# Feed-forward of a latent-attention block in two phases: the down product as one Strassen product

## The chip, the cores and the metric

The kernel runs on one core of a Trainium2 chip as a single program. The metric is the time of that program on the device in microseconds (us), as the median of several runs. A profile of one execution gives the span of its instructions, the busy time of each engine (PE is TensorE, PEld its weight loads, DVE VectorE, ACT ScalarE, POOL GpSimd) and the queue of SyncE (SP), which issues all the transfers between memory and the chip.

## What is computed

All arithmetic is float32. After the attention part the feed-forward part takes 896 rows (8 x 112) of 1,024 features:

```python
logits = jnp.einsum('bsh,he->bse', hidden_states, gate_w)
routing_weights, selected_experts = jax.lax.top_k(logits, K)
h = jax.nn.relu(jnp.einsum('bsh,hi->bsi', hidden_states, up_w)) ** 2
shared_out = jnp.einsum('bsi,ih->bsh', h, down_w)
...
routed_out = jnp.einsum('bsl,lh->bsh', moe_out, fc2_w)
return _layernorm(shared_out + routed_out, ln_gamma, ln_beta)
```

`up_w` is 1,024 x 2,048 and `down_w` is 2,048 x 1,024. The attention part, the layer norm ahead of it and the expert products stand before this part and are not touched.

## The kernel before

Precision: each float32 operand is kept as two parts in a reduced format, hi (a rounded copy, written by ACT) and lo (value minus hi, written by POOL or DVE). A product is three matmuls (`three`: hi x hi, lo x hi, hi x lo) that add up in one PSUM bank, so every tile costs three matmuls per 128 features of depth.

Feed-forward, up: the 2,048 hidden features are worked off in 8 pairs (`F_PAIRS`) of 2 x 128. In each pair the up product is a Strassen product in the Winograd form: 7 units (`up_product(p, n)`, n = 0 to 6, in the order `F_BLOCKS`: A11, S2, A12, S3, S1, A22, S4), each of 12 matmuls with 448 columns (448 of the 896 rows). The weight operand of a unit is a 128 x 512 block or a sum of blocks. For one pair the work beside PE is:

- SP loads four blocks A11, A21, A22, A12 of 256 KB (`load_up`), each when the unit that last needed its buffer has its lo.
- POOL makes the four block sums in place (`up_sum`, steps 1 to 4: S1, S2, S4, S3) and the lo of all 7 units (`up_lo`), in one fixed order.
- ACT writes the hi of each unit (`up_hi`, two slots `F_UNIT`), copies the first product, and writes the rectified and the rounded hidden block.
- DVE adds the products (`up_combine`, 7 times), squares the hidden block and writes its lo.

Feed-forward, down: between the units of the next pairs PE runs the down product of finished pairs, `down_product(c, r, eh, pairs)`: for each of 7 row tiles of 128 and each half `eh` of the 1,024 outputs, 12 matmuls with 512 columns per pair, added by DVE to `Y` (`add_down`). The list `WEAVE` says how many of these groups stand behind each unit (two as a rule), so most units are followed by 24 matmuls of down work. The last two pairs' down products follow the last unit, and the layer norm of the rows runs behind them. The seven `routed_product` groups (12 matmuls with 512 columns each) stand in the first pair.

The order on each engine is written out by hand; engines wait for each other by counting semaphores, and every queue is worked off in order, SP's too.

```python
def three(out_ap, w, a, first, last):
    pe.matmul(out_ap, w[0], a[0], start=first, stop=False)
    pe.matmul(out_ap, w[1], a[0], start=False, stop=False)
    return pe.matmul(out_ap, w[0], a[1], start=False, stop=last)
```

## Time and profile before

| | |
|---|---|
| median of 3 runs (lowest to highest) | 1729.22 us (1728.54 to 1729.24) |
| the profiled execution: its time / its span | 1728.13 us / 1726.3 us |
| granted TensorE clock, mean | 0.999 of full speed |
| busy: PE / DVE / POOL / ACT | 1717.0 / 965.2 / 950.4 / 701.8 us |
| feed-forward part (first up unit to the last matmul) | about 1411 to 1719.5 us |

The span runs from the first instruction to the last; the time lies 1.83 us above it. A PE that is busy is not at its peak, since matmuls are pipelined: what counts in the text is the distance from the start of one matmul to the start of the next.

### The profile page before, as it was taken

The numbers are of one execution on the slowest core, as the hardware profiler recorded it, in microseconds if no ns is written. First come the engines' busy times: TensorE is split into PE (matmuls) and PEld (weight loads), VectorE is DVE, ScalarE is ACT, GpSimd is POOL, SyncE is SP. The second block draws the span as 40 slices with busy tenths as digits, with TensorE's granted clock in tenths as the row PEclk, the third lists the DMA queues.
The fourth block names the chain that finished last, engine by engine and source line by source line (L and its number), as shares of the span: only waits on it lengthen the run. The fifth ranks groups of instructions, "written<-read, shape, count | busy, mean of one in ns | idle before, by whom it ended". The sixth has DMA issues, their size and how long they took to land.

```text
span 1726.3 us, 24782 instructions
## 1 busy us (share of the span) xinstructions
PE 1717.0 (99%) x8599; PEld 1516.2 (88%) x8599; DVE 965.2 (56%) x1503; ACT 701.8 (41%) x1361; POOL 950.4 (55%) x779
## 2 busy tenths in 40 slices
PE   9999999999999999999999999999999999999998
PEld 8988998899999988988998898889888988888886
DVE  3611112743434357874887588657657465555568
ACT  4311212233334357743873377337613233333332
POOL 2365552445555549874767476735535245465553
PEclk9999999999999999999999999999999999999999
DMA  8788875566668758844773477334222212111124
GB/s 272 228 290 283 292 245 214 176 192 214 217 217 253 225 189 302 293 129 136 242 236 113 142 250 218 121 99 148 82 86 88 95 31 73 56 61 49 56 78 172
DMA packets 196951, 296.31 MB, mean 172 GB/s; under 512 B 19344, under 2 KB 159120, under 8 KB 195984
## 3 DMA queue, kind: packets, MB, share of 16 engines
q1 hardware_dynamic: 196880, 295.41, 52.4%
q8 instruction: 38, 0.62, 0.2%
q14 instruction: 33, 0.27, 0.0%
HBM read 197.10 MB, written 98.27 MB: 171 GB/s over the span
## 4 chain that ended last, share of the span: by engine, by line
PE 96%; DVE 2%; DMA 0%; ACT 0%; POOL 0%; issue 0%; SPq 0%; DVEq 0%; ACTq 0%; POOLq 0%
PE bank L2061 30%; PE bank L2062 29%; PE bank L2063 29%; PE bank L2285 5%; PE bank L2147 1%; DVE mid_region L1764 1%; DVE y_region L1783 0%; DMA mid_region<-k_latents_scratch 0%; PE bank L2426 0%; PE bank L2133 0%; PE bank L2104 0%; DVE tile_region L1771 0%; DVE y_region L1771 0%; POOL tile_region L994 0%; PE bank L2140 0%
## 5 line engine op out<-in xcount | busy, mean ns | idle before, releaser
L994 POOL TENSOR_TENSOR tile_region<-tile_region,small 128x487 f32<-128x487 f32 x224 | 221.1, 1024 | 72.9 <-DVE small L1647 72.7
L2061 PE MATMUL bank<-mid_region 128*128 128x488 f32 (+4 forms) x532 | 218.7, 411 | 0.1
L2062 PE MATMUL bank<-mid_region 128*128 128x488 f32 (+4 forms) x532 | 199.8, 376 | 0.0
L2063 PE MATMUL bank<-mid_region 128*128 128x488 f32 (+4 forms) x496 | 185.4, 374 | 0.0
L2061 PE MATMUL bank<-mid_region,act_region 128*125 128x512 f32 (+2 forms) x434 | 168.7, 389 | 0.1
L2062 PE MATMUL bank<-mid_region,act_region 128*125 128x512 f32 (+2 forms) x434 | 168.5, 388 | 0.0
L1271 ACT ACTIVATE tile_region<-bank,small 128x487 f32<-128x487 f32 x224 | 153.8, 687 | 30.3 <-DVE small L1651 30.3
L960 POOL TENSOR_TENSOR slab_raw<-slab_raw 128x256 f32<-128x256 f32 x128 | 98.7, 774 | 120.2 <-DMA slab_raw<-in_slabs 112.6
L1303 ACT ACTIVATE mid_region<-bank 125x512 fp32r<-125x512 f32 x224 | 136.7, 613 | 54.5 <-PE bank L2285 54.5
L1651 DVE TENSOR_REDUCE small<-bank 128x1 f32<-128x487 f32 x224 | 145.7, 652 | 20.6 <-PE bank L2063 20.6
L1702 DVE TENSOR_TENSOR mid_region<-bank,mid_region 125x512 fp32r<-125x512 f32 x224 | 151.4, 681 | 9.3 <-ACT mid_region L1303 9.3
L2063 PE MATMUL bank<-mid_region,act_region 128*125 128x512 f32 (+2 forms) x404 | 156.5, 387 | 0.0
L2285 PEld LDWEIGHTS bank<-ident,tile_region 128*125 128x125 f32 x896 | 131.4, 187 | 15.5 <-POOL tile_region L994 1.6
L978 POOL TENSOR_TENSOR slab_split<-slab_raw,slab_split 128x512 fp32r<-128x512 f32 x64 | 87.6, 1371 | 94.2 <-ACT slab_split L1221 94.2
L2285 PE MATMUL bank<-ident,tile_region 128*125 128x128 f32 x896 | 134.4, 273 | 0.8 <-DVE mid_region L1702 0.8
L2063 PE MATMUL bank<-act_region,mid_region 128*128 128x376 f32 (+3 forms) x340 | 118.4, 348 | 0.0
L1783 DVE TENSOR_TENSOR y_region<-y_region,bank 128x512 f32<-128x512 f32 x105 | 68.7, 681 | 83.0 <-PE bank L2063 82.2
L1522 DVE TENSOR_TENSOR small_region<-bank,small_region 128x375 fp32r<-128x375 f32 (+1 forms) x40 | 22.4, 563 | 161.9 <-ACT small_region L1137 161.8
L2061 PEld LDWEIGHTS bank<-mid_region 128*128 128x128 f32 (+2 forms) x532 | 100.5, 189 | 10.1 <-issue 1.9
L2062 PEld LDWEIGHTS bank<-mid_region 128*128 128x128 f32 (+2 forms) x532 | 101.1, 190 | 6.7
L2061 PE MATMUL bank<-act_region,mid_region 128*128 128x376 f32 (+3 forms) x304 | 104.9, 345 | 0.0
L2062 PE MATMUL bank<-act_region,mid_region 128*128 128x376 f32 (+3 forms) x304 | 104.1, 343 | 0.0
(256 smaller groups left out, 4351.7 us busy)
## 6 DMA issues: line engine op xcount, KB each, us to landing
slab_raw<-in_slabs SPq DMA_DIRECT2D x112, 256.0 KB, 3.6
q_scratch<-y_region SPq DMA_DIRECT2D x16, 1792.0 KB, 8.1
mid_region<-q_scratch SPq DMA_DIRECT2D x32, 896.0 KB, 6.7
slab_raw<-in_slabs SPq DMA_DIRECT2D x37, 512.0 KB, 3.5
weight_sums_scratch<-slab_raw SPq DMA_DIRECT2D x32, 512.0 KB, 4.2
v_scratch<-slab_split SPq DMA_DIRECT2D x8, 1536.0 KB, 7.8
slab_raw<-weight_sums_scratch SPq DMA_DIRECT2D x48, 256.0 KB, 4.7
mid_region<-v_scratch SPq DMA_DIRECT2D x32, 384.0 KB, 3.2
```

The lines of the kernel that those rows point to most:

```text
L960: pool.tensor_tensor(out, a, b, op).then_inc(s_sum[h], 1)
L978: pool.tensor_tensor(WB[n][1], WRAW[n], f32(WB[n][0]), ALU.subtract).then_inc(s_blo, 1)
L994: pool.tensor_tensor(PR[i][:, 0:KEYS], PR[i][:, 0:KEYS], rrow[:, i:i + 1].broadcast_to([P, KEYS]), ALU.mult).then_inc(s_pn, 1)
L1271: act.activation(PR[i][:, 0:KEYS], SB[RING[i]][:, 0:KEYS], ACT.Exp, bias=negmax[:, i:i + 1], accum_out=rowsum[:, i:i + 1]).then_inc(s_exp, 1)
L1303: act.activation(PT[0][0:KT, :, i * P:(i + 1) * P], TB[RING[i]][0:KT, :].rearrange("p (t n) -> p t n", t=4), ACT.Copy).then_inc(s_pth, 1)
L1651: dve.reduce_max(negmax[:, i:i + 1], SB[RING[i]][:, 0:KEYS], AX.X, negate=True).then_inc(s_max, 1)
L1702: dve.tensor_tensor(PT[1][0:KT, :, cols], TB[RING[i]][0:KT, :].rearrange("p (t n) -> p t n", t=4), f32(PT[0][0:KT, :, cols]), ALU.subtract ...
L1783: return dve.tensor_tensor(Y[:, r, cols_of(eh)], Y[:, r, cols_of(eh)], GB[i][:, :], op)
L2061: pe.matmul(out_ap, w[0], a[0], start=first, stop=False)
L2062: pe.matmul(out_ap, w[1], a[0], start=False, stop=False)
L2063: return pe.matmul(out_ap, w[0], a[1], start=False, stop=last)
L2285: last = pe.transpose(TB[RING[i]][0:KT, t * P:(t + 1) * P], PR[i][:, t * KT:(t + 1) * KT], ident[:, :])
```

## The change

The down product is taken out of the up phase. In phase one PE runs the 56 up units one behind the other (the seven routed groups stay in the first pair). The hidden values of all 2,048 features stay whole on chip in float32 (`HR`, eight pieces of 256 features). In phase two the down product is one Strassen product over 1,024 + 1,024 features: 7 products `D_PRODUCTS` in 4 steps `kp` each, with 4 or 3 row tiles (`D_TILES`: row tile 6 rides along as a fourth where it needs no sum), 25 tiles of 24 matmuls with 512 columns. The last tile is made in two halves of 256 columns.

What goes with it:

- The sums T1 to T4 of the down weight's blocks are made during phase one, in 16 chunks of 512 KB (`CHUNKS` gives pair, unit and buffer of each): SP loads a chunk in two transfers, DVE makes four sums of 128 x 256 one behind the other (`down_sums`), SP stores the chunk to memory. Phase two loads them as slabs of 512 KB (`load_down`, 28 slabs).
- The lo of the units S1 and A22 (n = 4 and 5) moves from POOL to DVE (`up_lo` in the vector program), counted by `s_ulo2`.
- From unit 8 on there are three slots for the hi and lo of a unit; ACT writes the hi of unit u + 3 behind unit u.
- The square of the hidden block is made by ACT in place; its hi and lo are made later, for each product of phase two (`chunk_hi`, `chunk_lo` 128 x 768, `ride_hi`, `ride_lo` 128 x 256), and DVE makes the sums S1 to S4 of the hidden values (`hidden_sum`, 128 x 768).
- ACT's `down_hi` and POOL's `down_lo` (128 x 1,024) now run 28 times in phase two, instead of 16 times in the up phase.
- DVE adds each product tile to one to four places of `Y` (`take`). The layer norm takes the row tiles in the order 3, 4, 5, 6, 0, 1, 2.

The diff, cut to its core:

```diff
-WEAVE = [[1] * 7, [0, 2, 2, 2, 2, 3, 3]] + [[2] * 7] * (F_PAIRS - 5) + [[2] * 7, [1] * 7, [1] * 7]
+ROUTED_WEAVE = (2, 2, 1, 1, 1, 0, 0)
+CHUNKS = ((1, 0, "Y"), (1, 1, "X"), (1, 3, "Z"), (1, 4, "V"), (1, 6, "Y"), (2, 0, "X"), (2, 3, "Z"), (2, 4, "V"),
+          (2, 6, "X"), (3, 0, "Y"), (3, 3, "Z"), (3, 5, "X"), (3, 6, "Y"), (4, 4, "X"), (4, 6, "Y"), (5, 5, "Y"))
+D_PRODUCTS = (("A11", "B11", 0), ("S1", "T1", 0), ("S2", "T2", None), ("A22", "T4", None), ("S3", "T3", None),
+              ("S4", "B22", 1), ("A12", "B21", 1))
+D_TILES = [(0, 1, 2) if h is None else (0, 1, 2, 3) for _, _, h in D_PRODUCTS]
...
+            def load_chunk(c):
+                buf, use, m, kp = CHUNK_BUF[c], CHUNK_USE[c], c % 4, c // 4
+                if use:
+                    sp.wait_ge(s_cst[buf], 16 * use)
+                to = CHUNK[buf].rearrange("p (e k c) -> p e k c", e=2, k=2)
+                for kh in range(2):
+                    blocks = slabs[down_base(kh):down_base(kh) + NK].rearrange("(e m) p c -> p e m c", e=2)
+                    sp.dma_start(to[:, :, kh, :], blocks[:, :, m, 2 * P * kp:2 * P * (kp + 1)]).then_inc(s_cld[buf], 16)
+            def store_chunk(c):
+                buf, use, m, kp = CHUNK_BUF[c], CHUNK_USE[c], c % 4, c // 4
+                sp.wait_ge(s_csum[buf], 4 * (use + 1))
+                sp.dma_start(td_d[:, kp, :, m, :].rearrange("t p c -> p t c"),
+                             CHUNK[buf].rearrange("p (t c) -> p t c", t=4)).then_inc(s_cst[buf], 16)
...
+                for n in range(7):
+                    u = 7 * p + n
+                    if more and n == 2:
+                        sp.wait_ge(s_ulo, lo_count(p, 3))
+                        load_up(p + 1, "A11")
+                    if more and n == 3:
+                        sp.wait_ge(s_ulo2, 2 * p + 1)
+                        load_up(p + 1, "A21")
+                    if more and n == 4:
+                        sp.wait_ge(s_ulo2, 2 * p + 2)
+                        load_up(p + 1, "A22")
+                    if more and n == 5:
+                        sp.wait_ge(s_ulo, lo_count(p, 6))
+                        load_up(p + 1, "A12")
+                    for c in range(len(CHUNKS)):
+                        if CHUNK_UNIT[c] + 2 == u:
+                            store_chunk(c)
+                        later = [i for i in range(c + 1, len(CHUNKS)) if CHUNK_BUF[i] == CHUNK_BUF[c]][:1]
+                        if CHUNK_UNIT[c] + 5 == u:
+                            for i in later:
+                                load_chunk(i)
+            sp.wait_ge(s_ulo, lo_count(F_PAIRS - 1, 3))
+            sp.wait_ge(s_ulo2, 2 * F_PAIRS - 1)
+            load_down(0)
+            sp.wait_ge(s_ulo2, 2 * F_PAIRS)
+            sp.wait_ge(s_ulo, lo_count(F_PAIRS - 1, 6))
+            for buf in "XYZV":
+                sp.wait_ge(s_cst[buf], 16 * CHUNK_BUF.count(buf))
...
             for p in range(F_PAIRS):
                 up_sum(1, p, "A21", "A21", "A22", ALU.add)
                 up_lo(p, 0)
                 up_sum(2, p, "A11", "A21", "A11", ALU.subtract)
                 up_lo(p, 1)
-                if p == 1:
-                    down_lo(0)
                 up_lo(p, 2)
                 up_sum(3, p, "A12", "A12", "A11", ALU.subtract)
                 up_sum(4, p, "A11", "A22", "A11", ALU.subtract)
                 up_lo(p, 3)
-                if 0 < p < F_PAIRS - 1:
-                    down_lo(2 * p - 1)
-                if p == F_PAIRS - 1:
-                    down_lo(2 * F_PAIRS - 4)
-                up_lo(p, 4)
-                up_lo(p, 5)
                 up_lo(p, 6)
-                if 0 < p < F_PAIRS - 2:
-                    down_lo(2 * p)
-            for d in range(2 * F_PAIRS - 3, 2 * F_PAIRS):
+            for d in range(D_SLABS):
                 down_lo(d)
...
-                if u >= 2:
+                if 2 <= u < 8:
                     act.wait_ge(s_up, u - 1)
...
+                if u > 8:
+                    act.wait_ge(s_up, u - 2)
+                act.activation(up_slot(u)[0], F_BLOCK[F_SRC[name]], ACT.Copy).then_inc(s_uhi, 1)
...
+            def hidden_block(p, n, i):
+                m, h = F_TILES[n]
+                act.wait_ge(s_upc, 7 * p + {2: 2, 4: 4, 5: 6, 6: 7}[n])
+                if i == 0:
+                    for buf, first in (("V", 3), ("Z", 4), ("X", 5), ("Y", 6)):
+                        if p == first:
+                            act.wait_ge(s_cst[buf], 16 * CHUNK_BUF.count(buf))
+                to = HR[p][:, m, h * HALF:(h + 1) * HALF]
+                act.activation(to, F_FIRST if n == 2 else F_SUM, ACT.Relu).then_inc(s_relu, 1)
+                act.wait_ge(s_relu, 4 * p + i + 1)
+                act.activation(to, to, ACT.Square).then_inc(s_sq, 1)
...
-                    if n < 5 or not last:
-                        up_hi(p + (n >= 5), (n + 2) % 7)
...
+                    for v in (u + 2,) if u < 5 else (7, 8) if u == 5 else (u + 3,):
+                        if v < UNITS:
+                            up_hi(v // 7, v % 7)
...
+                    if last and n == 5:
+                        chunk_hi(0, 0)
+                        chunk_hi(0, 1)
+                    if n in F_TILES:
+                        hidden_block(p, n, list(F_TILES).index(n))
+                    if last and n == 5:
+                        down_hi(0)
...
+            chunk_hi(0, 2)
+            ride_hi(0, 0)
+            chunk_hi(0, 3)
+            down_hi(1)
+            for kp in range(1, 4):
+                ride_hi(0, kp)
+            down_hi(2)
+            for q in range(6):
+                for kp in range(4):
+                    chunk_hi(q + 1, kp)
+                    if q == 4:
+                        ride_hi(1, kp)
+                    down_hi(4 * q + kp + 3)
+            for d in range(27, D_SLABS):
...
+            def down_sums(c):
+                buf, use = CHUNK_BUF[c], CHUNK_USE[c]
+                dve.wait_ge(s_cld[buf], 32 * (use + 1))
+                W11, W21, W12, W22 = [part(CHUNK[buf], 256 * k, 256) for k in range(4)]
+                for n, (out_, a, b) in enumerate([(W11, W12, W11), (W12, W22, W12), (W22, W22, W11), (W21, W22, W21)]):
+                    if n:
+                        dve.wait_ge(s_csum[buf], 4 * use + n)
+                    dve.tensor_tensor(out_, a, b, ALU.subtract).then_inc(s_csum[buf], 1)
...
+                    if n == (2 if p == 0 else 1):
+                        up_lo(p, 4)
+                    if n == (3 if p == 0 else 2):
+                        up_lo(p, 5)
+                    for c, r in woven(p, n):
+                        routed_rows(c, db(c), r, 1)
+                    if 7 * p + n in CHUNK_UNIT:
+                        down_sums(CHUNK_UNIT.index(7 * p + n))
+                    if p == F_PAIRS - 1 and n == 5:
+                        chunk_lo(0, 0)
+                        chunk_lo(0, 1)
...
+            chunk_lo(0, 2)
+            ride_lo(0, 0)
+            chunk_lo(0, 3)
+            for kp in range(3):
+                hidden_sum("S1", kp, "A21", "A22", ALU.add)
+            for kp in range(1, 4):
+                ride_lo(0, kp)
+            hidden_sum("S1", 3, "A21", "A22", ALU.add)
+            for kp in range(4):
+                chunk_lo(1, kp)
+                hidden_sum("S2", kp, "S1", "A11", ALU.subtract)
...
+            def down_step(q, kp, i, out_ap, ms=slice(0, 4)):
+                pe.wait_ge(s_olo, 4 * q + kp + 1)
+                pe.wait_ge(s_dlo, 4 * q + kp + 1)
+                act, rows = D_OP[4 * (q % 2) + kp], slice(i * P, (i + 1) * P)
+                if i == 3:
+                    pe.wait_ge(s_rlo, 4 * D_PRODUCTS[q][2] + kp + 1)
+                    act, rows = D_RIDE[kp], slice(0, P)
+                w = [t.rearrange("p (m k c) -> p m k c", m=4, k=2) for t in d_slot(4 * q + kp)]
+                for k in range(2):
+                    last = three(out_ap, [act[l][:, k, rows] for l in range(2)], [w[l][:, ms, k, :] for l in range(2)],
+                                 kp == k == 0, kp == 3 and k == 1)
+                return last
+            pe.wait_ge(s_upc, UNITS)
+            for q in range(6):
+                banks = DB if q % 2 == 0 else GB
+                for kp in range(4):
+                    for i in D_TILES[q]:
+                        if kp == 0 and q >= 2:
+                            pe.wait_ge(s_dtake, taken(q - 2 if i in D_TILES[q - 2] else q - 4, i))
+                        last = down_step(q, kp, i, banks[i][:, :])
+                        if kp == 3:
+                            last.then_inc(s_dmm, 1)
+                    if kp < 3:
+                        last.then_inc(s_dmm, 1)
+            for i in D_LAST[:-1]:
+                pe.wait_ge(s_dtake, taken(0, i) if i == 3 else taken(4, i))
+                for kp in range(4):
+                    last = down_step(6, kp, i, DB[i][:, :])
+                last.then_inc(s_dmm, 1)
+            pe.wait_ge(s_dtake, taken(5, 0))
+            for h, dst in enumerate((DB[2], GB[0])):
+                for kp in range(4):
+                    last = down_step(6, kp, 2, dst[:, 0:256], slice(2 * h, 2 * h + 2))
```

## Rows read from the trace of the kernel before

**Rows 1.** The page: the busy line
```profile
PE 1717.0 (99%) x8599; PEld 1516.2 (88%) x8599; DVE 965.2 (56%) x1503; ACT 701.8 (41%) x1361; POOL 950.4 (55%) x779
```

**Rows 2.** The page: the chain that ended last, by engine
```profile
PE 96%; DVE 2%; DMA 0%; ACT 0%; POOL 0%; issue 0%; SPq 0%; DVEq 0%; ACTq 0%; POOLq 0%
```

**Rows 3.** One up-phase window: length, busy of PE, PEld, DVE, ACT, POOL; clock, DMA
```profile
1600.00:1650.00 50.00, 50.00 (x235) 43.94 (x234) 28.66 (x41) 16.58 (x27) 28.74 (x20) 1.00 0.23 74
```

**Rows 4.** PE in order of time: start, duration; one unit, one down group, the end
```profile
1549.93 0.36 PE L2061 MATMUL bank<-mid_region,slab_split 128*128 128x448 f32 x1
...
1552.37 0.39 PE L2061 MATMUL bank<-small_region,slab_split 128*128 128x512 f32 x1
...
1555.10 0.36 PE L2061 MATMUL bank<-mid_region,act_region 128*128 128x448 f32 x1
...
1716.44 0.28 PE L2061 MATMUL bank<-act_region,slab_split 128*128 128x256 f32 x1
...
1719.20 0.28 PE L2063 MATMUL bank<-mid_region,act_region 128*128 128x256 f32 x1
```

**Rows 5.** POOL by line, 1420 to 1727 us: sums and lo parts (min/median/max ns)
```profile
L1078 POOL TENSOR_TENSOR slab_raw<-slab_raw x28: 1287/1296/1725, 1436.2 to 1660.6; 128x512 f32<-128x512 f32 x28
...
L1090 POOL TENSOR_TENSOR small_region<-tile_region,small_region x6: 2397/2398/2410, 1458.6 to 1637.2; 128x1024 fp32r<-128x1024 f32 x6
```

**Rows 6.** ACT and DVE by shape, 1430 to 1690 us: count, busy us, mean ns
```profile
L1419 ACT ACTIVATE slab_split<-slab_raw 128x512 fp32r<-128x512 f32 x25 | 15.7, 629 | 51.1 <-PE bank L2063 34.2 <-POOL slab_raw L1078 16.9
...
L1439 ACT ACTIVATE tile_region<-tile_region 128x448 f32<-128x448 f32 x24 | 13.8, 575 | 2.7 <-DVE tile_region L1951 2.6
...
L1429 ACT ACTIVATE mid_region<-tile_region 128x1024 fp32r<-128x1024 f32 x8 | 8.4, 1046 | 2.1 <-PE bank L2063 2.1
...
L1951 DVE TENSOR_TENSOR tile_region<-tile_region,bank 128x448 f32<-128x448 f32 x16 | 9.9, 619 | 18.0 <-PE bank L2063 12.9 <-issue 5.1
```

**Rows 7.** DMA issues, 1420 to 1700 us: KB each, median us to landing
```profile
tile_region<-in_slabs SPq DMA_DIRECT2D x15, 512.0 KB, 3.4
slab_raw<-in_slabs SPq DMA_DIRECT2D x28, 256.0 KB, 2.6
```

**Rows 8.** Hand-overs in order of time: POOL sum, ACT hi, POOL lo
```profile
1551.85 1.56 POOL L1078 TENSOR_TENSOR slab_raw<-slab_raw 128x512 f32<-128x512 f32 x1
...
1553.44 0.63 ACT L1419 ACTIVATE slab_split<-slab_raw 128x512 fp32r<-128x512 f32 x1 [2.21 <-POOL slab_raw L1078]
...
1554.15 1.29 POOL L1084 TENSOR_TENSOR tile_region_rounded<-slab_raw,slab_split 128x512 fp32r<-128x512 f32 x1 [0.74 <-ACT slab_split L1419]
```

**Rows 9.** DVE, then POOL in order of time: where their work overlaps
```profile
1410.58 2.01 DVE L1902 TENSOR_TENSOR tile_region<-tile_region,mid_region 128x1792 f32<-128x1792 f32 x1
1412.51 0.74 DVE L1875 TENSOR_SCALAR y_region<-bank,small 128x512 f32<-128x512 f32 x1
1413.17 2.46 DVE L1902 TENSOR_TENSOR tile_region<-tile_region,mid_region 128x1792 f32<-128x1792 f32 x1
...
1411.34 2.41 POOL L1084 TENSOR_TENSOR tile_region_rounded<-slab_raw,slab_split 128x512 fp32r<-128x512 f32 x1 [3.23 <-ACT slab_split L1419]
1414.21 2.57 POOL L1084 TENSOR_TENSOR act_region<-slab_raw,act_region 128x512 fp32r<-128x512 f32 x1 [0.46 <-ACT act_region L1419]
```

**Rows 10.** Windows at the start and behind the last matmul; columns as in rows 3
```profile
2.00:4.00 2.00, 2.00 (x7) 1.78 (x6) 0.00 (x0) 0.63 (x3) 2.00 (x9) 1.00 0.84 283
4.00:6.00 2.00, 2.00 (x8) 1.46 (x8) 1.15 (x2) 0.75 (x3) 0.85 (x1) 1.00 0.93 277
6.00:8.00 2.00, 2.00 (x14) 1.95 (x13) 1.49 (x3) 1.68 (x4) 0.00 (x0) 1.00 0.98 330
...
1721.00:1722.00 1.00, 0.00 (x0) 0.00 (x0) 0.87 (x3) 0.02 (x1) 0.00 (x0) 1.00 0.47 193
1722.00:1723.00 1.00, 0.00 (x0) 0.00 (x0) 1.00 (x2) 0.00 (x0) 0.00 (x0) 0.61 0.82 332
1723.00:1724.00 1.00, 0.00 (x0) 0.00 (x0) 0.85 (x2) 0.00 (x0) 0.00 (x0) 0.50 0.66 256
```

More of the change, by code:

```diff
@@ L293, in xattn_ffn, with raw_chunk, raw_ride, d_slot @@
+        def raw_chunk(name, kp):
+            at = {"A11": (0, 0), "S2": (0, 0), "S4": (0, 0), "S1": (0, 1), "S3": (0, 1), "A21": (0, 1), "A12": (1, 0), "A22": (1, 1)}
+            half, row = at[name]
+            return HR[4 * half + kp][:, :, 3 * P * row:3 * P * (row + 1)]
+        def raw_ride(half, kp):
+            return HR[4 * half + kp][:, :, 6 * P:7 * P]
+        def d_slot(d):
+            return D_W[4 if d == 24 else (d - (d > 24)) % 4]
         S_AT = SLOT
@@ L1431, in hidden_hi @@
[L1431 to L1445 removed]
+                if u == 8:
+                    act.wait_ge(s_ftlo, 3)
```

450 lines of the change are left out of this document (251 added, 199 removed).

## The prediction, made before the changed kernel was run

> **What bounds the kernel now.** First the busy line: PE works for 99% of the span, the others for 41 to 56% [rows 1]. Then the chain that ended last: 96% of it is PE's own work, DVE has 2%, transfers and queues nothing [rows 2]. So time is PE's list of matmuls, and the others are cover. The windows say the same of the up phase: in 50 us PE is never idle, while POOL works 28.7, DVE 28.7 and ACT 16.6 us [rows 3].
>
> In order of time a unit's first matmul starts at 1549.93, the down group behind it at 1552.37, the unit after at 1555.10 [rows 4]: a unit costs 2.44 us, a group of 12 matmuls with 512 columns 2.73. The last 24 matmuls (256 columns) stand 0.12 us apart [rows 4]. The feed-forward part is then 56 x 2.44 + 7 routed x 2.73 + 55 down groups x 2.73 + 24 x 0.12 = 136.6 + 19.1 + 150.2 + 2.9 = 308.8 us, and it lasts from about 1411 to 1719.5. With two groups behind it, a unit gives the other engines 2.44 + 5.46 = 7.9 us to prepare the next.
>
> **What it does to PE's own work.** Down work was 153.1 us. It becomes 24 tiles x 24 x 0.2275 + 48 x 0.12 = 131.0 + 5.8 = 136.8. **Term 1: -16.3 us.** It is won only if PE stays fed. The routed groups move within the first pair and cost the same.
>
> **The up phase without its cover.** A unit now has 2.44 us, a pair 17.1. Busy time is no obstacle: POOL has 4 sums and 5 lo parts of 1.29 us [rows 5] = 11.6; ACT 7 x 0.63 + 9 x 0.58 [rows 6] = 9.6; DVE 7 x 0.62 [rows 6] and two lo parts, 5.7. The order is. A POOL op follows the one before at once, or 0.08 us later if it needs its result; sum to hi takes 0.03, hi to lo 0.08 (1553.41 to 1553.44, 1554.07 to 1554.15) [rows 8]. Let unit 3 of a pair end at 0. ACT may write the hi of unit 6 (three slots), 0.2 to 0.8; POOL then runs lo 6, first sum, lo 0, second sum of the next pair: to 2.2, 3.5, 4.7, 6.1. Hi of unit 1 to 6.7, lo to 8.0; ACT has the two operations of the hidden block behind it, so hi 2 ends at 8.4, lo 2 at 9.8; sums three and four to 12.5, hi 3 to 13.2, lo 3 to 14.5. PE wants unit 3 at 6 x 2.44 = 14.6. So a quiet pair costs nothing, but this 14-us chain has no slack. The load of A22 has none either: hi and lo of unit 5 end 1.7 us after unit 2, the load lands 2.6 us later [rows 7], 0.2 us before POOL wants it.
>
> What is added to that is four DVE sums per chunk, 16 chunks, 12 of them in pairs 1 to 3. The trace of before has no such sum; the nearest rows are DVE operations with both inputs in SBUF. They and POOL's wait for each other: 1,792 columns take 2.01 us alone, 2.46 when POOL is at work; POOL's 1.29 us become 2.41 and 2.57 behind such an operation, each ending about 1.2 us after DVE lets go (1412.59 and 1415.63), while a DVE operation that reads a PSUM bank runs its usual 0.74 us beside POOL [rows 9]. From 448 columns in 0.62 [rows 6] and 1,792 in 2.01 [rows 9] a sum of 256 is 0.42 us. Lowest cost of one to the chain: nothing, if it falls into a gap of POOL. Highest: 0.42 to POOL, and for DVE a whole POOL operation of wait (1.29). I take 0.2 to POOL, and DVE waiting out what POOL has begun.
>
> For the change from pair 1 to 2 (chunks at units 3, 4, 6 and next 0): the sums behind unit 3 meet lo 6, sum, lo and end at 5.6 instead of 2.9. The combines of unit 4 follow, to 6.9, then the sums of the unit-4 chunk, of which the last waits for lo 1, to 10.0. Only now comes the combine of unit 5, 10.6. ACT waits for it with the hidden block, which stands ahead of hi 2: 11.9, hi 2 12.4 instead of 8.4. Lo 2 to 14.0 and two more chunks' sums between the sums of POOL, so lo 3 ends at 19.4: **4.8 us of idle PE**, some of it before unit 2, most before unit 3. Pair 2 to 3 has the same pattern. Its A22 load stands in SP's queue behind a chunk load and a chunk store: 1.75 MB from A11 on, at 0.8 us per further 256 KB [rows 7] 7.3 us, 2.6 late; mostly the same wait: 4.9. By the same count: pair 3 to 4 (units 3, 5, 6; A22 late by about 2) 2.9; 4 to 5 (units 4, 6; a chunk load ahead of A22) 1.7; 5 to 6 (one chunk) 0.5; 6 to 7 nothing. Pair 0 to 1 has two slots until unit 8: hi and lo of unit 7 start when unit 5 ends, 2.4 us later than in a settled pair, and two chunks: 3.0. **Term 2: +17.8 us**, bounds 3.0 (only the start) and 23 (each sum costs POOL its full 0.42: 56 further sums behind the start's two chunks x 0.22, halved for those that meet a gap, is 6, less what overlaps the late loads).
>
> **The joint between the phases.** PE's first down step needs slab 0 in both parts, and its hi stands on ACT behind two chunk operations and the hidden block of unit 5. Last unit ends at 0: combine 4 at -4.2, hidden block to -2.9, two hi of 768 columns (0.84 each, between 0.63 for 512 and 1.05 for 1,024 [rows 6]) to -1.3, hidden block to -0.1, hi of slab 0 (1.05) to 0.85, POOL's lo of 1,024 columns 2.40 [rows 5] to 3.3. **Term 3: +3.4 us.** At least 0.9, since PE waits for the last combine (0.62) anyway; at most 6, if POOL waits out two of DVE's 768-column operations (0.95 each by the same line). Slab 1 comes behind the last hidden block, three hi operations: lo at 7.5, wanted 5.46 after the start, 8.9. No second stall.
>
> **Phase two.** A step is 24 or 18 matmuls, 5.5 or 4.1 us. POOL's lo takes 2.4. Load 3.4 [rows 7] + hi 1.05 + lo 2.4 is 6.9 for one slab with two buffers, 3.5 per step. DVE per product: at most nine adds of 0.69, eight operations of 0.95 = 13.8 of 16.4 us; banks alternate, so adds have a whole product of time. ACT 2 us per step. Gamma and two x2 loads stand in SP's queue ahead of slab 6, which is wanted 30 us in. Hidden by the steps: 0; without that cover 1.3 per step would be POOL's worst excess (0.95 of DVE wait). The tail behind the last matmul (6.8 us in before) has the same operations: 0; the row tile ahead of it is scaled, added and stored in the last 5.8 us plus that tail, as before.
>
> **Sum.** 1728.1 (the profiled execution) - 16.3 + 17.8 + 3.4 = 1733.0. The median stands 1.1 above that execution, so **1734**.
>
> **Rivals.**
> A. The same, with the stalls within a third of the sizes above: 1734, from 1727 to 1740. Chance 0.45.
> B. Faster: DVE's sums fall into POOL's gaps (0.6 us before each hi, 3 us before lo 6), and the loads are in time. Place: the chain from lo 6 to lo 3. Then term 2 is 3.0: 1729.2 - 16.3 + 3.0 + 3.4 = 1719.3. It decides from the point where term 2 is below 12.9. For: POOL is busy for only two thirds of a pair, and DVE's sums may start while POOL waits for a hi. Against: the waits of rows 9, and the order on ACT. With half of the sums free it is 1724. Chance 0.31.
> C. The clock falls in the gaps. Behind the last matmul it goes from 1.00 to 0.61 in the fourth microsecond and to 0.50 (1.2 GHz) after [rows 10]; idle stretches of 3 us and more are what terms 2 and 3 are made of. At the start PE gets through 7 and 8 matmuls in 2 us, then 14 [rows 10]: four us at half pace, 2 us lost each time. With three falls and the stalls of A: 1734 + 6 = 1740, up to 1745. The rule of the Trainium skill stands against the change here (TensorE: Matmul & The Clock Gate, HAM oscillation): waits between bursts of matmuls let the clock fall back to half. By that rule the time is the 1740 of this rival, by the up phase's own rows, whose clock is 1.00 throughout [rows 3], 1734. Against: the gaps are mostly split between two units, and before never had one. Chance 0.14.
> D. Terms 2 and 3 just cancel term 1 (late loads without contention, or the reverse): 1729. Chance 0.10.
>
> **How the numbers follow.** Under 0.2% (3.5 us) is about what a measurement of this kernel can't tell from no change. Faster by more: all of B and a little of the low end of A, 0.33. Slower by more: C and most of A, 0.50. Same: D and a part of A, 0.17. Range for 8 in 10: from B, 1719, to C, 1744; A alone is 1727 to 1740.
>
> **What would show it.** Down matmuls 600 with 512 columns or their halves, and down phase from its first to its last matmul 137 to 138 us (term 1). In the windows of pairs 1 to 4 PE idle 2 to 5 us per pair, waiting for POOL's lo of units 2 and 3; the last pairs almost without idle (term 2). DVE's 256-column sums at a mean well over 0.42, POOL's 512-column operations at 1.4 to 1.6. One gap of 3 to 4 us, ended by POOL's lo of a 1,024-column slab (term 3). Granted clock under 1.00 in a slice: C. Wrong if PE waits in phase two, if the gaps end on DVE or a transfer, or if up units follow each other at 2.44 us throughout.

## The result: the change made the kernel slower by half a per cent

The changed kernel takes 1736.8 us (median of 6 runs, 1734.43 to 1742.97), the kernel before 1728.99 us beside it (6 runs, 1728.41 to 1729.93). The ratio is 1.0048, with a 95% interval of 1.0033 to 1.0064. The profiled execution took 1735.55 us, its span is 1733.8 us: 7.5 us more than before. The forecast was 1734 with a range of 1719 to 1744. Runs also spread more: 8.5 us between the fastest and the slowest, against 1.5 before. The kernel before can stray too: of 24 executions beside e11 to e13, two took 1734.2 us. By the granted clock the six executions are not alike: 0.998 for the two fastest (1734.43 and 1735.55, the profiled one), 0.996 or 0.997 for the other four.

The page of the kernel after: the busy line, and the chain that ended last by engine.

```profile
PE 1705.7 (98%) x8539; PEld 1502.7 (87%) x8539; DVE 1026.1 (59%) x1520; ACT 736.5 (42%) x1409; POOL 961.6 (55%) x775
...
PE 90%; DVE 3%; POOL 3%; DMA 2%; issue 1%; ACT 1%; SPq 0%; DVEq 0%; POOLq 0%; ACTq 0%
```

PE has 11.3 us less busy time than in [rows 1] and yet the span is longer. The chain says why: PE carries 90% of it instead of the 96% of [rows 2], and DVE, POOL and transfers, which had 2% together, now have 8%. Its waits in the feed-forward part (1411 to 1735 us) are these: us in total, times, longest.

```profile
PE bank L2289 <- POOL tile_region_rounded L1195: 8.9, 9, 1.7
PE bank L2289 <- POOL act_region L1195: 4.8, 4, 1.7
PE bank L2289 <- POOL act_region L1201: 3.1, 1, 3.1
PE bank L2289 <- DVE tile_region L2087: 0.8, 1, 0.8
PE bank L2289 <- DVE mid_region L2115: 0.2, 1, 0.2
```

L1195 is POOL's lo of an up block, L1201 its lo of a down slab, L2087 the combine. So 14 of the waits stand in the up phase (13 for a lo of POOL, one for a combine of DVE) and one of 3.1 us between the phases. The windows show the up phase settle with time (columns as in [rows 3]):

```profile
1455.00:1475.00 20.00, 17.04 (x82) 15.14 (x82) 18.43 (x26) 8.21 (x15) 11.56 (x9) 1.00 0.77 236
1475.00:1495.00 20.00, 15.93 (x77) 13.76 (x76) 15.16 (x24) 8.82 (x16) 10.37 (x9) 1.00 0.79 250
1495.00:1515.00 20.00, 17.95 (x88) 15.97 (x87) 19.33 (x25) 8.93 (x16) 12.27 (x10) 1.00 0.70 223
1515.00:1535.00 20.00, 17.40 (x84) 15.14 (x83) 14.61 (x19) 8.92 (x16) 11.53 (x10) 1.00 0.50 159
1535.00:1555.00 20.00, 18.81 (x93) 17.07 (x92) 12.54 (x16) 9.06 (x16) 13.51 (x11) 1.00 0.42 132
1555.00:1575.00 20.00, 19.06 (x93) 16.94 (x92) 7.46 (x10) 10.35 (x19) 13.06 (x11) 1.00 0.17 54
```

Before, PE was busy for all of such a window, and the transfers moved 74 GB/s [rows 3]. Now PE loses 2 to 4 us of 20 up to 1535, with DVE busy for 14.6 to 19.3 us of the window and transfers at 159 to 250 GB/s, and about 1 us after that. Busy shares alone don't say which of the two costs the time: PE loses least of these where DVE is busiest (1495 to 1515).

**Where one gap comes from.** The stretch around 1475 in order of time (start, duration), DVE, then ACT, POOL and PE:

```profile
1464.09 4.73 DVE L2105 TENSOR_TENSOR small_region_unrounded<-small_region_unrounded 128x256 f32<-128x256 f32 x4
1468.75 0.61 DVE L2087 TENSOR_TENSOR tile_region<-tile_region,bank 128x448 f32<-128x448 f32 x1
1470.00 0.62 DVE L2087 TENSOR_TENSOR tile_region<-y_region,bank 128x448 f32<-128x448 f32 x1 [0.65 <-ACT slab_split_unrounded L1535]
1470.54 3.75 DVE L2105 TENSOR_TENSOR tile_region<-tile_region 128x256 f32<-128x256 f32 x4
1474.21 3.98 DVE L2105 TENSOR_TENSOR act_region_unrounded<-act_region_unrounded 128x256 f32<-128x256 f32 x4
...
1470.00 0.58 ACT L1537 ACTIVATE slab_split_unrounded<-slab_split_unrounded 128x448 f32<-128x448 f32 x1
1470.48 0.61 ACT L1524 ACTIVATE slab_split<-slab_raw 128x512 fp32r<-128x512 f32 x1
...
1471.18 1.39 POOL L1195 TENSOR_TENSOR tile_region_rounded<-slab_raw,slab_split 128x512 fp32r<-128x512 f32 x1 [0.60 <-ACT slab_split L1524]
1472.65 2.79 POOL L1186 TENSOR_TENSOR slab_raw<-slab_raw 128x512 f32<-128x512 f32 x2
1476.18 1.27 POOL L1195 TENSOR_TENSOR tile_region_rounded<-slab_raw,tile_region_rounded 128x512 fp32r<-128x512 f32 x1 [0.74 <-ACT tile_region_rounded L1524]
...
1475.44 0.37 PE L2291 MATMUL bank<-mid_region,slab_split 128*128 128x448 f32 x1
1477.50 0.47 PE L2289 MATMUL bank<-act_region,tile_region_rounded 128*128 128x448 f32 x1 [1.69 <-POOL tile_region_rounded L1195]
```

To read from the end: PE stands for 2.06 us from start to start (0.20 is usual), until POOL's lo is there. POOL did lo, two sums and lo with nothing between but ACT's hi. The lo at 1471.18 began the chain late: its hi at 1470.48 stood on ACT behind the hidden block (1469.39 to 1470.58), that behind the combine of DVE at 1468.75, and that behind four sums which took 4.73 us. The next two chunks take 3.75 and 3.98 us. A chunk is four sums of 256 columns, which the forecast had at 0.42 us each.

**Between the phases** PE's starts are 1584.23 and 1587.74, then 0.43 apart:

```profile
1584.23 0.36 PE L2291 MATMUL bank<-mid_region,slab_split 128*128 128x448 f32 x1
1587.74 0.57 PE L2289 MATMUL bank<-act_region 128*128 128x512 f32 x1 [3.15 <-POOL act_region L1201]
1588.11 0.63 PE L2290 MATMUL bank<-act_region 128*128 128x512 f32 x1
```

The windows of 1 us behind it show the granted clock at its lower level (1.2 GHz) for some 3 us:

```profile
1587.00:1588.00 1.00, 0.26 (x1) 0.29 (x2) 0.71 (x1) 1.00 (x3) 0.59 (x1) 0.98 0.00 0
1588.00:1589.00 1.00, 1.00 (x4) 0.70 (x4) 1.00 (x3) 1.00 (x2) 0.00 (x0) 0.50 0.23 43
...
1590.00:1591.00 1.00, 1.00 (x4) 0.81 (x3) 1.00 (x1) 0.17 (x1) 1.00 (x1) 0.50 0.47 164
1591.00:1592.00 1.00, 1.00 (x5) 0.78 (x5) 1.00 (x1) 0.97 (x1) 0.86 (x1) 0.81 0.00 0
```

Nine matmuls at 0.36 to 0.43 instead of 0.2275 cost 1.7 to 1.8 us. The last matmul starts at 1726.10, 7.7 us before the end of the span; before it was 7.1 (1719.20 [rows 4], span 1726.3).

### The profile page after: what moved, and what is told of

It is laid out like the page before. It is cut to its first block, busy times and chain, and to the rows that moved or that the text cites. A ratio compares the mean times of both kernels' runs of the same rounds, so it can differ in the third digit from the quotient of the medians.

```text
span 1733.8 us, 24758 instructions
## 1 busy us (share of the span) xinstructions
PE 1705.7 (98%) x8539; PEld 1502.7 (87%) x8539; DVE 1026.1 (59%) x1520; ACT 736.5 (42%) x1409; POOL 961.6 (55%) x775
## 4 chain that ended last, share of the span: by engine, by line
PE 90%; DVE 3%; POOL 3%; DMA 2%; issue 1%; ACT 1%; SPq 0%; DVEq 0%; POOLq 0%; ACTq 0%
PE bank L2289 28%; PE bank L2290 28%; PE bank L2291 28%; PE bank L2513 5%; POOL slab_raw L1186 1%; DMA slab_raw<-in_slabs 1%; PE bank L2375 1%; POOL tile_region_rounded L1195 1%; DVE act_region_unrounded L2105 1%; POOL act_region L1195 0%; DMA mid_region<-k_latents_scratch 0%; DVE tile_region L2105 0%; PE bank L2654 0%; PE bank L2361 0%; DVE slab_split_unrounded L2125 0%
## 5 line engine op out<-in xcount | busy, mean ns | idle before, releaser
L1102 POOL TENSOR_TENSOR tile_region<-tile_region,small 128x487 f32<-128x487 f32 x224 | 221.1, 1024 | 73.2 <-DVE small L1787 73.1
L2289 PE MATMUL bank<-mid_region 125*128 125x448 f32 (+4 forms) x608 | 248.3, 408 | 0.5 <-DMA mid_region<-k_latents_scratch 0.3
L2290 PE MATMUL bank<-mid_region 125*128 125x448 f32 (+4 forms) x608 | 229.4, 377 | 0.0
L2291 PE MATMUL bank<-mid_region 128*128 128x488 f32 (+4 forms) x572 | 215.0, 376 | 0.0
L2289 PE MATMUL bank<-mid_region,act_region 128*125 128x512 f32 (+3 forms) x434 | 168.5, 388 | 1.7 <-POOL act_region L1195 1.7
L2290 PE MATMUL bank<-mid_region,act_region 128*125 128x512 f32 (+3 forms) x434 | 168.3, 388 | 0.0
L2291 PE MATMUL bank<-mid_region,act_region 128*125 128x512 f32 (+3 forms) x404 | 156.3, 387 | 0.0
L2291 PE MATMUL bank<-act_region,mid_region 128*128 128x376 f32 (+3 forms) x366 | 128.5, 351 | 0.0
L2289 PEld LDWEIGHTS bank<-mid_region 128*128 128x128 f32 (+2 forms) x608 | 114.7, 189 | 13.8 <-issue 2.7
L2290 PEld LDWEIGHTS bank<-mid_region 128*128 128x128 f32 (+2 forms) x608 | 115.4, 190 | 9.6
L2291 PEld LDWEIGHTS bank<-mid_region 128*128 128x128 f32 (+2 forms) x572 | 107.5, 188 | 14.9
L2289 PE MATMUL bank<-act_region,mid_region 128*128 128x376 f32 (+3 forms) x330 | 115.0, 348 | 0.0
```

Source lines behind the costliest of these rows:

```text
L1102: pool.tensor_tensor(PR[i][:, 0:KEYS], PR[i][:, 0:KEYS], rrow[:, i:i + 1].broadcast_to([P, KEYS]), ALU.mult).then_inc(s_pn, 1)
```

## The experiments

All were run beside the kernel before; its median was 1728.5 to 1729.0 in each set of runs. "Up phase" below is the time from the start of the last matmul ahead of the first gap to the start of the last up matmul, in the profiled execution: 135.40 us in the changed kernel (1448.83 to 1584.23).

**e1: neither sums nor traffic.** No chunk is loaded, summed or stored; plain blocks of the down weight stand for T1 to T4, so the output is another.

```diff
+                i, j = {"T1": (1, 1), "T2": (1, 2), "T3": (2, 1), "T4": (2, 2)}.get(name, (int(name[1]), int(name[-1])))
+                rows = row_slab(down_base(i - 1), kp, j - 1)
             def load_chunk(c):
+                return
```

(the same return in store_chunk and down_sums)

> The changed kernel without the 16 chunks: no chunk loads, no sums on VectorE, no stores; phase two loads plain blocks of the down weight in place of T1 to T4 (same size and shape), so the down product is not the reference's. The idle time of PE between up units, 17.4 us in the changed kernel, should fall to that of the start, about 3 us, if the chunks cause the rest (term 2): time about 1736.8 - 14 = 1722.5, faster than before. If the 14-us chain of POOL and ACT is itself too long without cover, idle time stays above 8 us and the time above 1727. The joint (3.3 us idle, then 3 us of half clock) stays.

Measured: 1722.32 us (1721.34 to 1723.83), ratio 0.9964 (0.995 to 0.9978). The up phase is 121.42 us (1448.61 to 1570.03), 14.0 less than in the changed kernel. The gap between the phases stays, 3.50 us, here without a fall of the clock; a second gap in phase two, 0.56 us in the changed kernel, is 2.17 us here (at 1582.91, ended by DVE's lo of a ride row). So the two-phase order as such is worth 6.7 us by the medians, and the building of T1 to T4 costs 14.5, more than that.

**e2: traffic without sums; e3: sums without traffic.** e2 loads and stores every chunk, unsummed. e3 loads each of the four buffers once, stores nothing, and does all 64 sums. Both outputs are others.

```diff
 # e2
-                sp.wait_ge(s_csum[buf], 4 * (use + 1))
+                sp.wait_ge(s_cld[buf], 32 * (use + 1))
             def down_sums(c):
+                return
 # e3, in load_chunk
-                if use:
-                    sp.wait_ge(s_cst[buf], 16 * use)
+                if use:
+                    return
```

> The chunks are loaded and stored as in the changed kernel, but VectorE makes no sums, so T1 to T4 are unsummed blocks and the down product is not the reference's. Theory S (the sums, through the waits between VectorE and POOL and the order on ACT, cost most): only the late loads of A22 stay, idle between up units 5 to 7 us, time about 1726. Theory L (the transfers ahead of A22 in the queue cost most; POOL waited 15.9 us for loads in the changed kernel's up phase): idle 12 us or more, time 1731 to 1735.

> VectorE makes all 64 sums, but each chunk buffer is loaded once only and nothing is stored; phase two loads plain blocks in place of T1 to T4, so the down product is not the reference's. Theory S: VectorE's 256-column sums stay at 0.8 to 1.0 us each, hi of unit 2 still stands behind the hidden block of unit 5; idle between up units 12 to 15 us, time 1731 to 1734. Theory L: without the transfers idle falls to 5 us and the time to 1725.

Measured: e2 1734.39 us (1732.34 to 1737.03), ratio 1.0035 (1.0022 to 1.0047), up phase 132.47 us. e3 1737.21 us (1735.46 to 1738.54), ratio 1.0046 (1.0029 to 1.0063), up phase 137.05 us. Over e1 that is 11.1 and 15.6 us. The clock fell once in the up phase of e2 and three times in that of e3, behind gaps of 2.41 to 2.48 us; each time 9 matmuls took 0.375 instead of 0.21, 1.5 us. Without these, traffic alone costs 9.5 us, sums alone 11.1, both together 14.0: they don't add up. That fits two delays of the same chain of POOL, where what waits for one finds the other already done.

**e11: the same sums, with one input from PSUM.** As e3, but the second input of each sum comes from an idle bank, so that it subtracts whatever stands there.

```diff
-                    dve.tensor_tensor(out_, a, b, ALU.subtract).then_inc(s_csum[buf], 1)
+                    dve.tensor_tensor(out_, a, DB[3][:, 0:256], ALU.subtract).then_inc(s_csum[buf], 1)
```

> As the run with sums only (each chunk buffer loaded once, nothing stored, plain blocks of the down weight in place of T1 to T4), but each of the 64 sums of VectorE takes its second input from a PSUM bank that is idle then; it computes the chunk minus what stands in that bank. So only the kind of operand changes: as many operations, as many columns, in the same places of the list. If the up phase waits because VectorE with two inputs in SBUF and GpSimd hold each other up: a sum takes about 0.4 us (mean of sums only: 0.84 to 0.95), GpSimd's 512-column operations about 1.3, the idle of the up phase falls from 16 us to that of the start plus a few tenths per pair, 3 to 6 us, no clock fall in the up phase, and the time is 1723 to 1727. Rival: the cost is VectorE's own time and its place in the order (the combines stand behind the sums): then sums still delay the combine of unit 5, half or more of the idle stays, and the time is 1730 to 1737.

Measured: 1724.21 us (1722.34 to 1725.82), ratio 0.9972 (0.9961 to 0.9983), up phase 123.23 us: 1.8 over e1 instead of 15.6. The same 64 operations at the same places of DVE's list, of the same width, cost 13 us less of the median, of which some 4.5 us are e3's three falls of the clock in the up phase (e11 has none there). The sums of one buffer kind by shape, count, busy us and mean ns; first e3, then e11:

```profile
L2104 DVE TENSOR_TENSOR act_region_unrounded<-act_region_unrounded 128x256 f32<-128x256 f32 x32 | 30.4, 951 | 0.8
```

```profile
L2104 DVE TENSOR_TENSOR act_region_unrounded<-act_region_unrounded,bank 128x256 f32<-128x256 f32 x32 | 13.4, 419 | 0.8
...
L1185 POOL TENSOR_TENSOR slab_raw<-slab_raw 128x512 f32<-128x512 f32 x28 | 36.3, 1295 | 3.7 <-DMA slab_raw<-in_slabs 1.9
```

POOL's sums have a mean of 1,344 ns in e3 and 1,295 in e11. The contention is shown, and so is who pays: DVE's sums on average more than double, an operation of POOL grows by 4%. The averages hide two kinds of sum. In the changed kernel, by duration in ns (min/median/max) and first and last start:

```profile
L2105 DVE TENSOR_TENSOR act_region_unrounded<-act_region_unrounded x32: 413/426/1569, 1456.7 to 1527.9; 128x256 f32<-128x256 f32 x32
L2105 DVE TENSOR_TENSOR tile_region<-tile_region x24: 414/1385/1580, 1449.4 to 1549.6; 128x256 f32<-128x256 f32 x24
```

Of the 64 sums 31 take about 0.42 us. The other 33 (0.6 to 1.6 us) all started while a POOL operation was running, and each ended about 0.28 us after that operation: they waited it out. The Trainium skill (SBUF — State Buffer, SBUF: two separate sides) says that a VectorE operation with two inputs in SBUF and a GpSimd operation share a port pair as an exclusive lock, so that the later one waits for the whole of the other. The 33 sums that waited out POOL's operation agree with that, and so do the sums with one input in PSUM, which pay nothing.

**e4 and e9: the order at the joint.** e4 lets ACT do hi of slab 0 ahead of the second chunk and of the last hidden blocks. e9 also moves DVE's second chunk lo behind the last combine and the rows' lo ahead of the S1 sums.

```diff
 # e4, ACT
                     if last and n == 5:
                         chunk_hi(0, 0)
+                        down_hi(0)
                         chunk_hi(0, 1)
...
-                    if last and n == 5:
-                        down_hi(0)
 # e9, DVE as well
                         chunk_lo(0, 0)
+                    if p == F_PAIRS - 1 and n == 6:
                         chunk_lo(0, 1)
```

> Only the order around the joint changes: ACT writes the hi of down slab 0 behind the first chunk instead of behind the second chunk and the hidden block of unit 5, and the hi of slab 1 ahead of two chunks; VectorE takes the row tile 6 part first. Same result as the changed kernel. Term 3 says the gap of 3.5 us between the starts of the last up matmul and the first down matmul falls to 1.5 to 2, perhaps with up to 1 us at the second step. If the fall of the clock hangs on that gap, the down phase begins at 0.23 us per matmul and 1.8 us more are won: time 1736.8 - 3 = 1733.5. If the clock falls all the same, 1735.

> The joint again. In the first attempt the gap was ended by the last combine on VectorE, which stood behind the lo of the second chunk (1.8 us each beside POOL's slab lo). Now that lo stands behind the combine, and the small row tile 6 parts stand ahead of the sums S1. Same result as the changed kernel. Gap between the starts of the last up and first down matmul 3.5 to about 1.7 us, the clock stays at 1.00 there, no gap of 0.5 us or more at the fourth tile: 1736.8 - 1.8 - 1.8 - 0.4 = 1732.8. If the gap stays over 2.5 us, another wait takes its place and the time stays within 1 us of 1736.8.

Measured: e4 1736.65 us (1735.61 to 1738.11), ratio 1.0049 (1.0032 to 1.0066): no gain. The gap is 3.15 us and is now ended by DVE's combine (L2086, 2.79 of wait), which stands behind two chunk operations, the second of which waits out POOL's lo (2.68 us instead of 0.95); one wait took the place of the other, and the clock fell behind this gap too. e9: 1733.45 us (1731.3 to 1738.83), ratio 1.0032 (1.0017 to 1.0046). The gap is 1.90 us, the clock stays up, and the second small gap of the changed kernel (0.56 at 1598.75, ended by DVE's ride lo) is gone. A new gap of 0.87 us stands at 1661.49. The gap between the phases is 1.6 us shorter, and phase two 1.3 (1.8 of clock and 0.3 won, 0.6 lost); the medians differ by 3.4, more than that 2.9, with a spread of 7.5 us in e9.

**e5 and e6: two orders in the up phase.** e5 puts ACT's hidden block of unit 5 behind the hi of the next unit. e6 puts the chunk transfers of units 2 and 3 behind the load of A22 in SP's queue.

```diff
 # e5, ACT
-                    if n in F_TILES:
-                        hidden_block(p, n, list(F_TILES).index(n))
+                    if n == 6 and not last:
+                        hidden_block(p, 5, list(F_TILES).index(5))
+                    if n in F_TILES and (n != 5 or last):
+                        hidden_block(p, n, list(F_TILES).index(n))
 # e6, SP
-                    for c in range(len(CHUNKS)):
-                        if CHUNK_UNIT[c] + 2 == u:
+                    for at in () if n in (2, 3) else (u - 2, u - 1, u) if n == 4 else (u,):
+                        for c in range(len(CHUNKS)):
+                            if CHUNK_UNIT[c] + 2 == at:
```

> One change of order on ScalarE: the hidden block of unit 5 stands behind the hi that is written at unit 6, no longer ahead of it. Same result as the changed kernel. The prediction's working says the sums delay the chain mainly through this place (4 us in pairs with a chunk at unit 4). If so, idle between up units falls from 17.4 to 10 to 13 us and the time from 1736.8 to about 1731. If the late loads of A22 cover the same wait (the transfers alone cost 9.8 us of idle, the sums alone 11.7, both 14.2 more than neither), it gains 1 to 2 us.

> One change of order on SyncE's queue: chunk loads and stores that stood between the loads of A11 and A22 go behind the load of A22. Same result. POOL's wait for the loads (15.9 us in the changed kernel) falls to 6 to 9 us. Theory L: the time falls by 5 us or more, to 1731. Theory S (the sums alone hold 11.7 us): it falls by 2 us, to 1734.5.

Measured: e5 1735.48 us (1734.31 to 1737.05), ratio 1.0039 (1.0025 to 1.0054), up phase 133.96: 1.4 less in that execution, within the spread of the medians. Its longest gap, 3.97 us at 1485.78, comes after POOL has waited 5.1 us for a late A22, and the clock falls behind it (about 1.5 us), so that without this fall the up phase is 2.9 us shorter. e6 1739.62 us (1735.37 to 1740.49), ratio 1.0055 (1.0038 to 1.0072), up phase 138.44. POOL's wait for loads goes from 10.9 to 3.1 us (the 15.9 of the expectation is not what this view gives), but now DVE waits for its chunks (3.6 us in all), and gaps of 2.57, 2.67 and 2.48 us stand in their place. Behind each of them the clock falls, where the changed kernel's longest up-phase gap is 2.06 us and none has a fall: that is about 4.5 us of the 138.44. So the longer up phase of e6 is the falls; without them it would be about 1.5 us shorter than the changed kernel's. Its interval overlaps that of the changed kernel (1.0033 to 1.0064), so a loss isn't shown either. Alone neither order is a measurable gain.

**e10, e12, e13: the orders together.** e10 is e9, e5 and e6. e12 adds one wait on DVE, e13 is e12 without e6.

```diff
+            dve.wait_ge(s_dlo, 4)
             for kp in range(4):
                 chunk_lo(1, kp)
```

> The three changes of order together: hidden block of unit 5 behind hi on ScalarE, chunk transfers behind A22 on SyncE, the joint as in the run before. Same result. If sums and late loads overlap, as the two half-experiments suggest (9.8 and 11.7 against 14.2), removing both waits together gains more than each alone: idle between up units 17.4 to 8 us, the joint 4 us: about 1724, faster than both kernels. If the chain on POOL is lengthened by the sums as such, idle stays at 12 us or more and the time above 1728.

> The three orders together, and VectorE waits for GpSimd's lo of slab 3 before it starts with the chunk of the second product. If GpSimd was starved in the run without it (its 1,024-column lo took 8.05 us instead of 2.40 while VectorE ran 768-column operations without a gap): no gap of 3.9 us at 1600, no fall of the clock behind it, 4 to 5 us less in that execution, and the median falls from 1731.75 to 1727 to 1730. Rival: the 8.05 us had another cause (a late load, a wait of ScalarE): the gap stays, or returns at another slab, and the time stays at 1731 to 1733.

> The order at the joint and the hidden block behind hi, with the same pause of VectorE, but the chunk transfers at their old places in the queue (moving them alone made VectorE wait for chunks). If that move is on balance a loss: 1728 to 1731, below the run with all orders and the pause. If the late load of A22 costs more than VectorE's waits for chunks: 1731 to 1734, above it.

Measured: e10 1731.75 us (10 runs, 1728.48 to 1736.57), ratio 1.0017 (1.0007 to 1.0027). Its profiled execution, 1735.61, had a gap that the changed kernel has not: 3.92 us at 1599.67, ended by POOL's lo of slab 3. That is where the pause comes from. DVE and POOL there, in order of time:

```profile
1594.22 0.94 DVE L2127 TENSOR_TENSOR mid_region_unrounded<-mid_region_unrounded,tile_region 128x768 f32<-128x768 f32 x1
1595.09 0.95 DVE L2127 TENSOR_TENSOR small_region_unrounded<-small_region_unrounded,act_region_unrounded 128x768 f32<-128x768 f32 x1
1595.96 0.94 DVE L2112 TENSOR_TENSOR mid_region<-slab_split_unrounded,mid_region 128x768 fp32r<-128x768 f32 x1
...
1600.31 0.95 DVE L2127 TENSOR_TENSOR mid_region_unrounded<-mid_region_unrounded 128x768 f32<-128x768 f32 x1
...
1595.40 8.05 POOL L1202 TENSOR_TENSOR mid_region<-slab_raw,mid_region 128x1024 fp32r<-128x1024 f32 x1 [3.79 <-ACT mid_region L1553]
```

Six more operations of DVE follow each other at 0.87 us, each at its undisturbed 0.95, and POOL's operation ends 2.2 us after the last of them, about its own 2.4 us. That is as if it had done nothing in between. With the pause (e12) the same operation takes 2.91 us, the gap and the fall of the clock behind it are gone, and the median is 1730.01 us (11 runs, 1727.72 to 1731.37), ratio 1.0005 (0.9996 to 1.0014). e13 has 1732.14 us (11 runs, 1730.09 to 1737.37), ratio 1.002 (1.001 to 1.0031): with the other orders in place, the move of the chunk transfers is worth 2 us by the medians (the intervals overlap by little), though alone (e6) it was not a gain.

**e14: the whole change, with the sums freed.** e13, and ACT copies three of a chunk's four parts into two banks that are idle in the up phase. Each sum then has one input in PSUM. The output is that of the changed kernel.

```diff
+            def chunk_to_banks(c):
+                ...
+                to = DB[2 * (c % 2)], DB[2 * (c % 2) + 1]
+                act.activation(to[0][:, :], part(CHUNK[buf], 0, 512), ACT.Copy).then_inc(s_cpy, 1)
+                act.activation(to[1][:, 0:256], part(CHUNK[buf], 768, 256), ACT.Copy).then_inc(s_cpy, 1)
...
-                for n, (out_, a, b) in enumerate([(W11, W12, W11), (W12, W22, W12), (W22, W22, W11), (W21, W22, W21)]):
+                for n, (out_, a, b) in enumerate([(W11, W12, P11), (W12, P22, W12), (W22, P22, W11), (W21, W22, P21)]):
```

> The whole change again, with the order at the joint, the hidden block behind hi and the pause, and with the sums freed of the contention: ScalarE copies three of the four parts of a chunk into two PSUM banks that are idle in the up phase (columns 0 to 511 and 768 to 1,023, two operations behind the hi of that unit), and each sum takes one input from there. If the two costs of the up phase overlap as they did alone (traffic 9.8 us, sums 11.7, both 14.2, clock falls taken out), freeing the sums wins 4.4 us of the 1732.1 of the same kernel without it: 1727.7, in 1725 to 1730; sums at 0.42 us, waits for GpSimd's lo halved, the wait for the late block A22 left. Rival: ScalarE's two copies (1 us per chunk) hold up the hi of the next units, and what is won on VectorE is lost there: 1730 to 1734, with the lo operations waiting longer for ScalarE.

Measured: 1729.53 us (11 runs, 1728.78 to 1731.07), ratio 1.0004 (0.9995 to 1.0013): 2.6 under e13 instead of 4.4, and a spread of 2.3 us instead of 7.3. The sums take 0.42 us; ACT's two copies 0.58 and 0.37. The contention is gone, and PE still waits for POOL in the up phase, which lasts 131.56 us against e13's 132.82. First the sums of one shape, then the waits:

```profile
L2120 DVE TENSOR_TENSOR act_region_unrounded<-act_region_unrounded,bank 128x256 f32<-128x256 f32 x16 | 6.7, 421 | 10.1 <-ACT bank L1614 9.3
```

```profile
PE bank L2305 <- POOL tile_region_rounded L1196: 6.4, 9, 0.9
PE bank L2305 <- POOL act_region L1196: 3.8, 5, 1.5
...
POOL slab_raw L1187 <- DMA slab_raw<-in_slabs: 8.3, 5, 3.0
```

The waits for POOL's lo were to be halved; they are 10.2 us instead of the 12.2 of e13 (13.7 in the changed kernel). POOL waits 8.3 us for late blocks, and DVE's sums wait 18.5 us for ACT's copies (9.3 in the shape shown). How much of the 4.4 the copies took back isn't shown. e14 has the chunk transfers at their old places; together with e6's move it wasn't tried. No version with T1 to T4 in place beats the kernel before; e12 and e14 can't be told from it.

## Why the prediction was right, step by step

**Term 1 (-16.3 us)** holds within half a microsecond. Phase two runs from 1587.74 to 1726.10, 138.4 us. The forecast's 136.8 with the 1.8 of the clock and the 0.3 of the gap at 1598.75 is 138.9; POOL and the transfers are hidden in it, as the forecast had it.

**Term 2 (+17.8 us)** was 17.4 by the gaps (starts further apart than the usual 0.20, and 0.1 at the matmul behind each). By pairs of the up loop 2.35, 4.0, 4.35, 2.4, 3.0 and 1.2 where 3.0, 4.8, 4.9, 2.9, 1.7 and 0.5 were forecast. The path is the predicted one: a DVE that is late with a combine, the hidden block on ACT, the hi behind it, POOL's chain lo, sum, sum, lo. Two things inside it were not. First, the split of the contention. I let DVE wait out what POOL had begun, and that is what 33 sums did. But I also took 0.2 us per sum to POOL, and its 512-column operations at 1.4 to 1.6 us. They have means of 1.30 to 1.33 us: POOL paid about 1.6 us in all on its 64 operations (84.3 us against 82.7 in e1, where DVE makes no sums). DVE paid the rest, 58.0 instead of 26.9 us for its 64 sums by these rows:

```profile
L2105 DVE TENSOR_TENSOR act_region_unrounded<-act_region_unrounded 128x256 f32<-128x256 f32 x32 | 27.3, 852 | 1.1 <-DMA act_region_unrounded<-in_slabs 0.3
L2105 DVE TENSOR_TENSOR tile_region<-tile_region 128x256 f32<-128x256 f32 x24 | 24.4, 1016 | 0.6
L2105 DVE TENSOR_TENSOR small_region_unrounded<-small_region_unrounded 128x256 f32<-128x256 f32 x8 | 6.3, 791 | 0.2
```

Second, the loads. I had A22 late in three pairs and mostly under the same wait. It is late in five of them: POOL waits 10.9 us for blocks, up to 3.4 at a time, 2.9 of it in pair 4 to 5, where 3.0 us of gaps stand for the forecast's 1.7. Which of the two made these isn't shown: traffic alone leaves 2.1 us there (e2), the sums alone 2.6 (e3). Blocks of 256 KB take 3.1 us to land instead of 2.6 [rows 7], beside chunk loads of 4.2 to 4.8. Traffic alone is worth 9.5 of the 14.0 us (e2). The sum came out right because the two overlap, as the forecast had it for A22 in pair 2 to 3 ("mostly the same wait"), and in part by luck: the first four pairs were forecast 2.5 us too long and the last two 2.0 too short.

**Term 3 (+3.4 us)** was 3.3, ended by POOL's lo of slab 0, with ACT's hi of it at 1584.12 as counted. e9 shows that 1.6 of it was order.

**What the sum left out.** One fall of the clock, 1.8 us, which the forecast had in rival C; the fourth tile's 0.3 us; and 0.6 us in the tail, where DVE's first centring waits for POOL's last row (1.26 instead of 0.75 us at 1727.64, with POOL busy from 1726.01 to 1728.35). I had put the tail at 0. With them: -16.3 + 17.4 + 3.3 + 1.8 + 0.3 + 0.6 = +7.1; the spans differ by 7.5.

**The rivals.** B (the sums fall into gaps, 1719) would have needed what e11 does to the operands: with 0.42-us sums and without traffic the time is 1724. It failed on the contention and on the loads, each of which would have been enough (e2, e3). C had its mechanism right. The profiled execution had one fall, not three, with a mean clock of 0.998. But e6's profiled execution had three falls with 0.996, the clock of three others of the changed kernel's six, so an estimate from these two is about three falls there, which is C's count. At 1.5 to 1.8 us a fall that is most of why the median, 1736.8, lies 2.8 above the forecast; the forecast priced a fall at 2 us and left it out of the sum. D is what e12 and e14 arrive at: e14 takes 3.8 us from term 2 (up phase 131.56 instead of 135.40), 1.6 from term 3 and 1.3 from phase two (1.8 of clock and 0.3 won, a new gap of 0.6 at 1659.35), but its profiled execution came to the up phase 1.0 us later: the spans differ by 5.8, the medians by 7.3.

## What to carry to other kernels

Work that is moved out of a long cover into a short one must be priced on the engine that it delays, not by its busy time: here 27 us of sums, on an engine that is busy for 7.5 of 20 us without them, cost 11 us of PE's time by themselves (e3), and with the transfers 14, where the two-phase order without them had won 6.7 (e1). Look at the kinds of operands first: where VectorE and GpSimd are both on the path, a sum with one input in PSUM costs 0.42 us and one with both in SBUF 0.8 to 1.0 on average, and that change alone was 13 us between e3 and e11, falls of the clock included. When two chains are late together, change them together: e5 and e6 measured no gain each and e9 3.4 us, the set 5 to 7 us (e10, e12). And count the falls of the clock in a profile before blaming an order for its time (e6).

## What the runs showed of the hardware

**GpSimd can be starved.** VectorE operations with both inputs in SBUF that follow each other without a wait kept a GpSimd operation of 2.4 us from its work until they ended: 8.05 us (e10). Where each VectorE operation waits for the one before (the sums), it is VectorE that loses: a sum that starts beside a GpSimd operation waits it out, and 0.42 us become up to 1.6. The Trainium skill (SBUF — State Buffer, SBUF: two separate sides) gives the pair to whoever starts first, for one instruction. In this trace GpSimd stays outside through a row of such instructions.

**The length of a gap alone doesn't decide whether the clock falls.** It fell behind gaps of 2.41 to 2.67 us (e2, e3, e6) and of 3.15 to 3.97 (the changed kernel, e2, e3, e4, e5, e10, e11), and not behind 2.38 (e13), 2.77 (e12) or the same 3.50 in e1 and 3.51 in e6. Most falls cost 1.5 to 1.8 us (8 or 9 matmuls at half pace); two cost 2.6 (e10, at 1603.59) and 3.0 (e3, between the phases), with 12 and 14 such matmuls. By the rule of the Trainium skill (TensorE: Matmul & The Clock Gate, HAM oscillation) waits between bursts let the clock fall back to half; these runs agree that they may, and show that the same wait may not. More falls in some executions than in others explain part of the spread (8.5 us in the changed kernel, 2.3 in e14), but not all: at 0.996 the changed kernel took 1736.44 and 1742.97, and e10 at 0.999 took 1728.48 and 1734.31. What makes the rest stays open.
